# Setup spread over the first chunk-steps, x requested earlier, gates of a tile loaded behind their own stores, and a new written-out order

## What is computed

```python
h = _layernorm(x) * (1 + ca) + sa
h = rmsnorm(h) * norm_w
v = (h @ W_v.T).reshape(B, T, H, M)                       # H = 8 heads, M = 16
gates = softmax((h @ W_a.T).reshape(B, T, H, M, M + 1))   # 2176 numbers a token
def step(state, inp):                                     # 512 steps, one behind the other
    At, ut = inp                                          # At = gates[..., 1:], ut = gates[..., 0] * v
    new = jnp.einsum('bhij,bhj->bhi', At, state) + ut
    return (new, new)
x = x + ga * (h_in + h_out @ W_out.T)
h = _layernorm(x) * (1 + cb) + sb
# router: logits, top 4 of 8, softmax over them; each expert: gate_up 128 -> 512, SiLU, down 256 -> 128
x = x + gb * experts(h)
```

## Time and profile before

| | before |
|---|---|
| median of 3 runs | 864.83 us (863.77 to 866.02) |
| the profiled execution's own time | 862.44 us |
| its span, from the first instruction to the last | 860.7 us |
| busy share of the span: TensorE matmul, VectorE, ScalarE, GpSimd | 72%, 82%, 63%, 80% |
| mean granted clock of TensorE, as a share of 2.4 GHz | 0.867 |

### The profile page before, as it was taken

The page is one execution under the profiler, slowest core; times in us unless marked ns, Lnnn a source line. Parts: engine busy times, 40 slices in busy tenths (PEclk is TensorE's granted clock), DMA queues, the critical chain, the costliest instruction groups (busy, mean ns, idle before and its releaser), DMA issues.

```text
span 860.7 us, 11466 instructions
## 1 busy us (share of the span) xinstructions
PE 621.6 (72%) x2762; PEld 460.0 (53%) x2762; DVE 708.6 (82%) x1833; ACT 545.1 (63%) x1267; POOL 686.7 (80%) x731
## 2 busy tenths in 40 slices
PE   4743404597878787777869787877779695868886
PEld 3411102375666556555647556555646474757775
DVE  3452999999898998989998999989998999998431
ACT  3444323566767776768676776767676767556785
POOL 0498868798988998999988998989998888734454
PEclk9877756698897989999997999999979899789999
DMA  8008375555364546373553635553736455640000
GB/s 236 10 4 198 76 157 116 119 113 109 81 132 85 111 88 146 70 161 73 131 103 80 131 75 112 103 127 73 161 65 142 86 130 97 140 88 7 14 6 7
DMA packets 90659, 85.28 MB, mean 99 GB/s; under 512 B 42920, under 2 KB 87264, under 8 KB 88416
## 3 DMA queue, kind: packets, MB, share of 16 engines
q1 hardware_dynamic: 90592, 84.55, 46.3%
HBM read 44.66 MB, written 39.85 MB: 98 GB/s over the span
## 4 chain that ended last, share of the span: by engine, by line
POOL 51%; DVE 19%; issue 11%; PE 11%; ACT 4%; DMA 2%; SPq 1%; POOLq 0%; DVEq 0%; ACTq 0%
POOL ex L407 11%; POOL lg L414 8%; POOL fold L391 7%; DVE ps L852 6%; DVE prod L844 6%; POOL yacc L460 6%; POOL up L465 5%; PE ps L1156 4%; PE ps L1169 3%; DVE nmax L822 2%; POOL fold L394 2%; DVE act_t L918 2%; POOL ex L399 1%; PE ps L1143 1%; DMA gu_rows<-_L_ffn_gate_up_proj_dram 1%
## 5 line engine op out<-in xcount | busy, mean ns | idle before, releaser
L1156 PE MATMUL ps<-h2t,wgu 128*128 128x256 f32 x1024 | 279.4, 421 | 7.8 <-ACT up L622 7.8
L1156 PEld LDWEIGHTS ps<-h2t,wgu 128*128 128x128 f32 x1024 | 211.2, 213 | 60.1 <-issue 18.2
L844 DVE TENSOR_TENSOR prod<-gates,ps 64x272 f32<-64x272 f32 x512 | 215.6, 421 | 20.9 <-DMA gates<-gate_dram 14.4
L852 DVE TENSOR_REDUCE ps<-prod 64x16 f32<-64x272 f32 x512 | 219.6, 429 | 8.9
L1143 PE MATMUL ps<-wl,ht 128*128 128x512 f32 (+1 forms) x320 | 171.7, 644 | 68.6 <-ACT lg L605 65.0
L1169 PE MATMUL ps<-wd,act_t 128*128 128x128 f32 x1024 | 153.1, 297 | 50.3 <-DVE act_t L918 50.3
L1169 PEld LDWEIGHTS ps<-wd,act_t 128*128 128x128 f32 x1024 | 142.4, 209 | 71.8 <-DVE act_t L918 58.9
L414 POOL TENSOR_TENSOR lg<-lg,nmax 128x1088 f32<-128x1088 f32 x64 | 130.2, 2038 | 13.4 <-DVE nmax L822 11.8
L918 DVE SCALAR_TENSOR_TENSOR act_t<-ps,up 128x512 f32<-128x512 f32 x128 | 87.3, 682 | 58.1 <-ACT ps L628 48.1
L407 POOL TENSOR_TENSOR ex<-ex,rz 128x1088 f32<-128x1088 f32 x64 | 130.4, 2039 | 5.2 <-DVE rz L835 3.0
L465 POOL TENSOR_SCALAR up<-up 128x512 f32<-128x512 f32 x128 | 78.6, 614 | 66.7 <-ACT up L622 60.3
(11 more groups left out here) (122 smaller groups left out, 609.4 us busy)
## 6 DMA issues: line engine op xcount, KB each, us to landing
gate_dram<-ex SPq DMA_DIRECT2D x256, 136.0 KB, 3.0
gates<-gate_dram SPq DMA_DIRECT2D x32, 1088.0 KB, 8.3
yt_tok<-y_dram SPq DMA_DIRECT2D x256, 8.0 KB, 5.5
xg<-in_L_attn_x_dram SPq DMA_DIRECT2D x32, 64.0 KB
y_dram<-ys SPq DMA_DIRECT2D x32, 64.0 KB, 2.2
out_dram<-res_out SPq DMA_DIRECT2D x32, 64.0 KB
wa_rows<-in_L_attn_W_a_dram SPq DMA_DIRECT2D x1, 1088.0 KB, 8.2
dn_rows<-in_L_ffn_down_proj_dram SPq DMA_DIRECT2D x1, 1024.0 KB, 12.8
```

The costliest lines, as they stand in the source:

```text
L844: nc.vector.tensor_tensor(prod[:, :].rearrange("p (i k) -> p i k", k=M1), gates[:, t, :].rearrange("p (i k) -> p i k", k=M1), state[:, (t ...
L852: nc.vector.tensor_reduce(state[:, t % TS, 1:M1], prod[:, :].rearrange("p (i k) -> p i k", k=M1), AX_X, ALU.add).then_inc(scan.sem, 1)
L1156: last = nc.tensor.matmul(gu_ps(m, k, which)[:, q * N:(q + 1) * N], wgu[:, k, rows + q * P:rows + (q + 1) * P], h2t[:, m % 2, :], start=Tr ...
```

## The change

1. Setup in parts. `whole` calls `setup(it)` ahead of `run` in every iteration. The five attention groups are made in iteration 1 (`WA_AT`), the other 13 in iteration 3 (`EXPERTS_AT`), in four PSUM banks instead of six. The gates' signs, the scaled norm weight and the start state move to iteration 1 as well. The first h waits for six steps of `mod` and not for the last.
2. x of chunk 0 is requested behind `c_rows` and `wmod_sb`, x of chunk 1 ahead of the biases and of the expert weights.
3. SP's list: store gates of a tile, store `ys`, load those gates, load y; then the same for the other tile.
4. The lists of all engines get another order within an iteration.

```diff
         def whole(run, setup):
             for it in range(NC + DEPTH - 1):
+                setup(it)
                 run(*[it - d if 0 <= it - d < NC else None for d in range(DEPTH)])
+        FREE_BANKS = (2, 3, 4, 7)
+        WA_AT, EXPERTS_AT = 1, 3
...
+            def setup(it):
+                if it != 0:
+                    return
+                sp.dma_start(c_rows[:, :], cond).then_inc(in_c, 16)
+                sp.dma_start(wmod_sb[:, :], w_mod).then_inc(in_wmod, 16)
+                load_x(0)
+                sp.dma_start(wa_rows[:, :, :], w_a.rearrange("(r j) d -> r j d", j=M1)).then_inc(in_wa, 16)
...
+                load_x(1)
...
+                sp.dma_start(gu_rows[:, :, :], gu_w.rearrange("e (k p) d -> p (e k) d", p=P)).then_inc(in_gu, 16)
...
                 for j in range(TILES):
+                    if e is not None:
+                        store_gates(e, j)
                     if s is not None:
-                        sp.wait_ge(ys_ok.sem, ys_ok.at(s, j + 1))
+                        store_y(s, j)
                     if e is not None:
+                        load_gates(e, j)
                     if s is not None:
+                        load_y(s, j)
...
             def run(a, g, e, s, p, m, o):
+                if o is not None:
+                    finish(o)
                 if e is not None:
                     fold_row(e, 0)
...
-                if o is not None:
-                    finish(o)
...
+                    norm_gates(e, 0, 1)
+                if m is not None:
+                    clamp_up(m, 2)
+                if e is not None:
                     gate_value(e, 1)
-                    norm_gates(e, 0, 1)
-                if m is not None:
-                    clamp_up(m, 2)
...
+                if it == EXPERTS_AT:
+                    pe.wait_ge(in_gu, 16)
+                    pe.wait_ge(in_dn, 16)
+                    pe.wait_ge(in_gub, 16 * 3)
+                    for i in range(N_GROUPS - N_WA):
+                        bank = FREE_BANKS[i % 4]
...
                 if p is not None:
                     route(p)
                 if m is not None:
+                    gate_up(m, 7)
                     down(m, 6)
```

More of the change, by code:

```diff
@@ L260, in adaln_block, with whole @@
         DEPTH = 7
-        def whole(eng, run):
-            def peeled(it):
+        def whole(run, setup):
+            for it in range(NC + DEPTH - 1):
+                setup(it)
                 run(*[it - d if 0 <= it - d < NC else None for d in range(DEPTH)])
-            for it in range(NC + DEPTH - 1):
-                peeled(it)
         WA_GROUPS = [(1, 4), (5, 4), (9, 4), (13, 4)]
@@ L284, in _ @@
         def _(sp):
[L285 to L294, removed]
             def load_x(a):
@@ new lines, in load_y @@
+            def load_y(s, j):
+                sp.wait_ge(y_st[j].sem, y_st[j].at(s, 16))
+                sp.sem_inc(passed_sp, 1)
+                if not is_first(s):
+                    sp.wait_ge(yt_ps.sem, yt_ps.at(s - 1, 1))
+                    sp.sem_inc(passed_sp, 1)
+                for b in range(B):
+                    sp.dma_start(yt_tok[b * TS:(b + 1) * TS, j, :].rearrange("t (h i) -> t h i", h=H),
+                                 y_dram[j, b].rearrange("h t i -> t h i")).then_inc(y_ld[j].sem, 16)
@@ L356, in _ @@
+            whole(run, setup)
             for j in range(TILES):
@@ L748, in run @@
                     router_exp(p)
-            whole(act, run)
+            whole(run, setup)
         @block.vector
@@ L1079, in run @@
                     between(3 * t + 2, a, g, e, p, m)
-            whole(dve, run)
+            whole(run, setup)
         @block.tensor
@@ L1228, in run @@
             def run(a, g, e, s, p, m, o):
+                if g is not None:
+                    logits(g, 0)
                 if m is not None:
@@ L1231, in run @@
                 if g is not None:
-                    logits(g, 0)
                     logits(g, 1)
+                if m is not None:
+                    gate_up(m, 1)
+                if g is not None:
                     logits(g, 2)
                 if m is not None:
-                    gate_up(m, 1)
                     turn_combine(m)
@@ L1263, in run @@
                     gate_up(m, 4)
-                if a is not None:
-                    turn_h(a, p)
                 if g is not None:
@@ L1269, in run @@
                     down(m, 3)
+                if a is not None:
+                    turn_h(a, p)
+                if m is not None:
                     gate_up(m, 5)
```

421 lines of the change are left out of this document (210 added, 211 removed).

## The result

| | before | after |
|---|---|---|
| median of the runs (4 of each) | 864.3 us (861.61 to 866.02) | 834.25 us (833.81 to 837.12) |
| ratio, with its 95% interval | | 0.9656 [0.9623, 0.9689] |
| the profiled execution's own time | 862.44 us | 833.87 us |
| its span | 860.7 us | 832.2 us |

The kernel is faster by 30 us (3.4%), where 834.0 was predicted.

The account below looks back on a forecast made before the run. VectorE and GpSimd were nearly full, neither bounding the kernel alone. A gain of 18.5 us before the scan's first product plus 12 in iterations 5 to 15 made 30.5, from the 864.8 us median to 834; range 824 to 848.

Parts of the forecast that it names:

- The fill: Start of the kernel until the scan's first product: 18.8 us gained by its summed terms, taken as 18.5.
- (1) The weights' setup: Start: only attention weights stand ahead of chunk 0's first logits, which come at 18.0 us, 16.0 earlier; bounds 17.1 and 20.
- The stall of chunk 1 and the `gate_value`: Start: chunk 1's later normalisation costs 0.8 us; `gate_value` no longer between tile 0's gate halves returns 0.5.
- (2) SP's order: Start: only tile 0's eight stores precede the first `gates` load, which leaves 3.1 us earlier.
- (3) The expert weights cost nothing: Iteration 3: VectorE's wait for the load covers 8.6 us of transposes and copies; at half clock up to 3.7 us lost.
- (4) SP's order in the full iterations: Full iterations: tile 1's stores behind y's load land in time, so nobody waits.
- (5) The full iterations: Iterations 5 to 15: reordered lists remove VectorE and GpSimd waits, 46.9 to 45.8 us each, 12 us in all.
- The walk: One full iteration followed through each engine's queue with measured durations: VectorE needs 45.7 us, GpSimd about 45.3 plus some tenths.
- Fill only (846 us): Rival: only the start gains, full iterations keep 46.9 us as waits are exchanged; 846 us, chance 0.2.
- Slower: Rival: `finish` before the first fold delays VectorE's row sum, up to 3.7 us per full iteration; 887 us, chance 0.05.
- The floor of 45.3 us: Rival: full iterations fall to GpSimd's work of 45.3 us and the end gains slightly; 826 us, chance 0.15.
- The signs: Observations listed beforehand: right if first product at 64 to 67 us, iterations 45.3 to 46.2; wrong if 47 or more.

Follow-up runs that it names:

- setup_only: Kernel before with the new setup and early requests of x, but the old lists of the computing engines and SP's old order: 848.79 us, ratio 0.9803.
- setup_and_sp: Kernel before with the new setup, requests of x and SP's new list; the four computing engines' lists stay old: 843.90 us, ratio 0.9752.
- experts_at_4: Kernel after with the expert weights made in front of iteration 4 instead of 3: 841.30 us, ratio 0.9725.
- finish_behind: Kernel after with `finish` moved back behind the first fold and first inverse root on GpSimd: 828.16 us, ratio 0.9565.
- lists_only: Kernel before with the new lists of GpSimd, ScalarE, VectorE and TensorE; setup and SP's list stay old: 855.12 us, ratio 0.9875.
- both_moves: Kernel after with `finish` behind the first fold and ScalarE weighing the last expert ahead of the first exponential: 850.66 us, ratio 0.9825.
- finish_acc: finish_behind with the accumulation of expert 2 put back behind the second inverse root on GpSimd: 827.37 us, ratio 0.9562.
- x_late: Kernel after with x of chunks 0 and 1 requested behind the attention weights and the small ones: 836.42 us, ratio 0.9668.

## Why the prediction was right, and where not

The total was right, 834.0 against 834.25 us, but that it is so close is luck. The fill gave 2.3 us more than predicted, iterations 5 to 15 gave 7.0 less, and the parts put at 0 gave 2.7 together. That leaves 2 us (a span of 832.2 where 830.2 was forecast), and they went because the profiled execution lay 0.4 us below the median of the runs after, and not 2.4 as I had reckoned with.

- **(1) The weights' setup: right.** First logits at 17.77 us (18.0 predicted), 16.2 us earlier. setup_only turned this into 16.25 us at the first product. The 0.9 us that I gave to the two loads of x ahead of `wa_rows` had another cause, though: `wa_rows` landed at 9.5 us and TensorE waited for `hh` until 11.3, which I had named for the upper bound; it cost 0.65 us. The stall of chunk 1 and the `gate_value` (-0.8 + 0.5) were not measured alone; all that the lists did in the fill is +0.52.
- **(2) SP's order: right in kind, too small.** 3.1 us predicted, 4.1 measured between setup_only and setup_and_sp (3.2 beside the new lists): the term left out that the load, requested without the second one behind it, takes 0.8 us less. The order took back 0.7 us in iteration 3, where tile 1's exponential waits for its stores; my "nobody waits" was reckoned for the full iterations, and holds there.
- **(3) The expert weights cost nothing: nearly right, with more cover than I gave.** They cost some 0.5 us between the first store and the load. "The cover left is 2 to 4 us" was 7.7 us: I had the transposes and copies end at 61 to 63 and they ended at 55.5 us, since TensorE reached them at 49.37, not at 52 to 54, and they took 6.1 us, not 8.6. My price of "up to" 3.7 us at half the clock was also not the most: it starts from 52 us, and from 54 the same sum gives 5.7. The half clock that I feared came in experts_at_4, behind 20 us in which TensorE was idle.
- **(4) SP's order in the full iterations: right**, 46.39 against 46.40 us.
- **(5) The full iterations: the step that failed.** 1.1 us each predicted, 0.45 measured (4.99 us in all, not 12). The waits that I named went, and so did nearly all of the Silu waits (14.8 to 1.8 us), which I had said nothing removes for certain; those in their place were priced nearly right (`xn` 0.6 for 1.0, `nm` 0.7 for 0.5). But I put down `finish` in front of the fold at nothing, since it "also stood in front of the second fold before". There it delays a sum that is asked for later, and the kernel before has no wait for a fold in its full iterations; in front of the first fold it made VectorE wait 11.0 us in all, 1.6 to 1.7 us in six of eleven iterations. The walk has a second fault: it gave VectorE 44.2 us of work, and without the listed waits it needed 44.1 before but 43.6 after. finish_behind takes `finish` away and comes to 45.90 us, beside the 45.8 of my walk, but that is in part luck: 43.8 of work, 1.3 for `xn` and `nm`, and 0.9 of waits for clamps and Silu, which the sum had not.
- **The rivals.** Fill only (846 us): not so; setup_and_sp is that case, and ran 843.9. Slower: its mechanism came, at 1.7 us and in every second iteration. Its price of up to 3.7 us was a sum of all three operations and the longest wait; two accumulations fewer ahead of the fold and a late slot 17 probably took off most of it; no run parts them. The floor of 45.3 us: short iterations of 45.5 us come near it. The floor itself was set too high, since in a 45.5-us iteration of finish_behind GpSimd still waits about 1.0 us (0.5, 0.3 and 0.2), which leaves 44.5.
- **The signs.** Of those of being right, the logits, the order of load and stores and the router's wait came; the first product (63.2 us) and the iterations (46.4 us) lie outside the ranges given. Of those of being wrong, three came: the wait for a fold, the exponential that waits for stores (once), and iterations of 47 us.
- **Iterations 16 to 18 and the end**, 0 predicted, 3.4 us measured, and not explained. The end is 58.8 us in setup_only too, which has the old lists, and 59.7 in lists_only. So the new lists are not needed for it. It goes rather with the granted clock there: 58.8 to 58.9 us in the six kernels that have 0.97 or 0.98 (after, with 0.98, is one), 59.3 to 59.9 in the five with 0.93 or 0.94, 60.9 in both_moves with 0.92. Only the kernel before falls out of that order, 60.4 at 0.95. Iterations 16 to 18 took from 121.6 to 128.5 us over all kernels. Both stay open, and so does why long and short iterations alternate, with a fold wait or without: that needs a delay carried from one iteration into the next, and no run here singled it out.

## What to carry to other kernels

In a kernel whose engines each carry out a fixed list, setup work is best placed where its consumer waits for a transfer anyway: here it cost some 0.5 us there, about as little one stage earlier, and 9.2 us one stage later, where it stood behind idle time of TensorE and the scan had no wait to cover it. When a step is moved to the front of a list, price it by when the result of what it is put ahead of is asked for, not by what it stood in front of before. Two moves that each gain by ending the same wait can lose together, because each takes away the other's cover: here 7.9 and 4.8 us gained alone, and 15 us lost together. And a wait that is gone from the list of waits need not be gained: look whether the instruction behind it has grown (here from 0.16 to 0.67 us). The best version here is finish_acc or finish_behind, 0.956 of the time before, 8 us below the changed kernel.

## What the hardware showed that I had not expected

- TensorE after 20.42 us of idle ran at a granted clock of 0.52 while busy for 6.36 of 6.40 us: 16 transposes in 3.61 us instead of 1.91 (experts_at_4).
- The same load of `wa_rows`, 1,088 KB, landed 5.4 us after its request in x_late, 6.4 in the kernel after and 8.2 in the kernel before.
- `nm` on VectorE, 128x2 elements, took 0.16 us in finish_behind and 0.67 in finish_acc, where it ended together with an accumulation on GpSimd.
- A load of gates of 1,088 KB took 8.1 us to its consumer with only eight stores beside it (setup_and_sp), and 8.9 us with the other tile's load requested right behind it (setup_only).
- The same lists gave iterations of 45.5 and 47.0 us, nearly in turn, with a granted clock of 0.93 in both kinds (232.6 to 279.6 and 279.6 to 325.2 us).
